# Reordering the opening of a one-core attention and feed-forward kernel: two quarters of q, the first bias loads, the mask's rows

## The chip, the cores and the metric

The kernel runs on one core of a Trainium2 chip. The metric is the device time of one execution in microseconds; the time of a kernel is the median of its runs. The engines work side by side and wait for each other by semaphores: TensorE (PE in the profile; PEld is its weight load), VectorE (DVE), ScalarE (ACT), GpSimd (POOL), and SyncE (SP), which here only issues DMAs.

## The reference

Eight sequences of 256 rows and 128 channels go through attention with 16 heads of 64 and a single k and v shared by the heads, then through a gated feed-forward layer with simulated 8-bit quantisation. The bias of the attention depends only on the distance between query and key and comes from a small network.

```python
xn = ln(x, g_norm)
q = (xn @ Wq).reshape(b, n, HEADS, DIM_HEAD).transpose(0, 2, 1, 3)
k, v = split(xn @ Wkv)                        # one head; a null key and a null value are put in front
q = l2norm(q) * q_scale;  k = l2norm(k) * k_scale
sim = einsum('bhid,bjd->bhij', q, k) * 8.0
bias = rel_pos_bias(...)                      # (heads, n, n), a Toeplitz matrix for each head
sim = where(causal, -inf, sim + [null_bias, bias])
sim = where(mask, sim, -inf)                  # mask of the keys, (b, n), all true in these inputs
out = softmax(sim) @ v
y = ln(out @ Wout, g_out)
x = x + ffn(y)                                # fake quantisation, w_gate, w_up, silu, w_down
```

## The kernel before

**Work and order.** The kernel is written by hand, engine by engine: each engine has one program, in the order of the code, and waits on named semaphores. No scheduler moves anything. After an opening that prepares the weights, the bias and the first sequence, a loop over 32 groups (8 sequences by 4 groups of 4 heads, `GB` = 4) does the attention; the last two groups are written out in `ending`, and the feed-forward part follows.

**The opening.** The q of the first sequence is made in four quarters (128 rows by 8 heads each; quarter `q` has rows `q % 2` and heads of half `q // 2`). A quarter goes through these steps: `q_make_first(q)` on PE (the product), `q_square(q)` on ACT, `q_norm2(q)` on DVE (the sum of squares for each head), `q_power(q)` on POOL (the power -1/2), `q_normalise(q)` on DVE (the product with it, into the one buffer `qn`), `qT_make(q)` on PE (four transposes of `qn` into the one bank `qT_ps`), and `qT_evac(q)` on DVE (the copy of `qT_ps` to `qT`). Quarter c may be normalised only when the transposes of quarter c - 1 are done, and be transposed only when the copy of quarter c - 1 is done. The first scores (`scores`, heads 0 and 1) need quarters 0 and 1, which are all rows of the first eight heads. `k_normalise` on DVE writes `kz`, which PE transposes (`kT_make`). `x_stats(1)`, `x_power(1)` and `x_normalise(1)` prepare the second sequence. `keep_busy(n, ...)` on PE transposes the unit matrix n times into a bank that nobody reads.

**The bias.** A table of 16 heads by 383 distances is computed, written to DRAM (`table_dram`) and read back by SP in eight DMAs of 256 KB: for each four heads, two blocks of keys. `ld_bias[k]` counts the two DMAs of heads 4k to 4k + 3. In group g of the first sequence, DVE waits for `ld_bias[g]` ahead of the first `score_pair`, which adds the bias to the scores of two heads and finds the row maxima, for ACT's `exponent`.

**The mask's rows.** `mrow` (one partition, bfloat16) holds an additive row of the mask for every sequence. ACT writes 2048 of its elements from the unsigned bytes of `mask_u`, DVE's `mask_tail` the other 1024. PE reads `mrow` only in the branch of the program that is taken when the mask has a zero; `least` picks the branch. With these inputs the other branch runs.

**GpSimd.** `x_power(0)`, `mlp_power(0)`, `mlp_power(1)`, `q_power(0, 0)` stand in that order; the `mlp_power`s belong to the small network that makes the bias. Later POOL multiplies the probabilities with the reciprocal sums (`normalise`).

Of the kernel before, what the change touches and what calls it, by code (L numbers as in the profile page):

```python
# [105 lines left out]
def held(eng, sem, value, passed):  # L106


    eng.wait_ge(sem, value)
    eng.sem_inc(passed, 1)  # L110
# [11 lines left out]
def build(nc, x, cond, mask, g_norm, Wq, Wkv, q_scale, k_scale, null_bias, w0, b0, g0, w1, b1, g1, w2, b2,  # L122
# [3 lines left out]
    with ExitStack() as ctx:  # L126
# [3 lines left out]
        def sem(name):  # L130
            return ctx.enter_context(nc.semaphore(name))
# [166 lines left out]
        ld_bias = [sem(f"ld_bias{k}") for k in range(4)]  # L298
        consts = sem("consts")
# [71 lines left out]
        def _(sp):  # L371
# [20 lines left out]
            for k in range(4):  # L392
                for blk in range(2):
                    toeplitz = bass.AP(table_dram, 4 * k * TABW + blk * P, [[1, P], [TABW, 4], [1, P]])
                    sp.dma_start(bias[:, 4 * k:4 * k + 4, blk * (P + 1) + 1:(blk + 1) * (P + 1)], toeplitz)\
                      .then_inc(ld_bias[k], 16)
# [29 lines left out]
        def _(pool):  # L426
# [25 lines left out]
            def x_power(n):  # L452
                power(mv[:, :, 1], rstd[:, :], n, 2, lambda: held(pool, x_aggr, 2 * (n + 1), pool_passed),
                      x_eps, x_rstd, True)
# [14 lines left out]
            def mlp_power(layer):  # L469
                power(mmv[:, :, 1], mrs[:, :], layer, 2, lambda: held(pool, mlp_aggr, 2 * (layer + 1), pool_passed),  # L470
                      mlp_eps, mlp_rstd, True)

            x_power(0)
            mlp_power(0)
            mlp_power(1)
# [62 lines left out]
        def _(act):  # L538
# [75 lines left out]
            q_square(3, q_ps0[3])  # L614
            act.wait_ge(ld_mask, 16)
            act.wait_ge(consts, 5)
            keys1 = mrow[0:1, :, 0:KEYS1].rearrange("p b (t k) -> p b t k", t=2)[:, :, :, 1:P + 1]
            mask_v = mask_u[:, :].rearrange("p (b n) -> p b n", b=B)[:, :, ::-1].rearrange("p b (t k) -> p b t k", t=2)
            act.activation(keys1, mask_v, ACT.Copy, scale=-NEG, bias=NEG).then_inc(mask_ready, 1)
            act.wait_ge(ld_v, 16 * 2)  # L620
            act.wait_ge(consts, 6)
            for a in range(2):
                for t in range(2):
                    dst = vnull[a * D:a * D + D, :, :].rearrange("p k h -> p (k h)")[:, 2 * a + t::2 * H + 4]
                    act.copy(dst, vcol[a * D:a * D + D, 0:1].broadcast_to([D, HP])).then_inc(vnull_ready, 1)

# [131 lines left out]
        def _(pe):  # L758
# [111 lines left out]
            keep_busy(4, idle)  # L870
# [5 lines left out]
            qT_make(0)  # L876
            q_make_first(3)
            keep_busy(6, idle)
            pe.wait_ge(null_a, 2)
            pe.wait_ge(kT_ready, 1)  # L880
            qT_make(1)
            keep_busy(6, idle)
# [314 lines left out]
        def _(dve):  # L1197
            def x_stats(n):
                for t in range(2):
                    dve.bn_stats(stat[:, t, :], X[:, 2 * n + t, :]).then_inc(x_stat, 1)  # L1200
                held(dve, x_stat, 2 * (n + 1), dve_passed)
                for t in range(2):
                    dve.bn_aggr(mv[:, t, :], stat[:, t, :]).then_inc(x_aggr, 1)

# [70 lines left out]
            def mask_tail():  # L1275

                mask_v = mask_u[:, :].rearrange("p (b n) -> p b n", b=B)
                dve.tensor_scalar(mrow[0:1, :, KEYS1 + 1:KEYS1 + P + 1], mask_v[:, :, ::-1][:, :, P:N], 1.0, -NEG,
                                  ALU.subtract, ALU.mult).then_inc(mask_ready, 1)

# [39 lines left out]
            mask_tail()  # L1320
            q_norm2(2, 2)
            qT_evac(0, 0, 0)
            q_normalise(1, 1, q_ps0[1])
            dve.wait_ge(ld_x, 16)
            x_stats(1)
            qT_evac(1, 1, 0)
            q_norm2(3, 3)
            q_normalise(2, 2, q_ps0[2])
# [97 lines left out]
            def group(s):  # L1426
# [16 lines left out]
                if s.at == 0:  # L1443
                    x_normalise(1)
                score_pair(heads(s.at)[2:4])
# [195 lines left out]
```

## Time and profile before

| | us |
|---|---|
| median of 3 runs | 286.36 |
| the three runs | 286.36, 286.25, 287.96 |
| profiled execution | 287.82 |
| its span in the profile | 285.9 |
| busy in it: PE, DVE, ACT, POOL | 260.6, 234.4, 223.5, 201.3 |

The rows of the trace are of the profiled execution, and count from the start of its span; 1.92 us of its time lie around the span. The profiled execution took 1.46 us more than the median of the runs, and lies near the slowest of them. In every row of a timeline the first two numbers are the start and the length in us; a row with x4 covers four instructions. "[0.94 <-DVE negmax L1379]" says that the engine had been idle for 0.94 us and what ended that. A DVE instruction can be shown starting up to 0.1 us before the one ahead of it has ended, so lengths of neighbours add up to a little more than the distance of their starts.

### The profile page before, as it was taken

To read this page: it belongs to the slowest core of one execution; us is meant where nothing else is said; L and a number is where in the kernel's file an instruction comes from. 1 tells how busy PE (TensorE), PEld (TensorE's weight loads), DVE (VectorE), ACT (ScalarE), POOL (GpSimd) and SP (SyncE) were. 2 spreads that over 40 slices of the span, in tenths; PEclk is the share of its full clock that TensorE was granted. 3 is DMA by queue.
4 is the path that set the end of the run, shared out by engine and by line. 5 is a ranking of instruction groups with operands and counts; after the bars stand their busy time and mean duration, and the time that the engine had idled before them with its cause. 6 is when DMAs were issued, how large, how long until landed. Compare 5 with 4: busy or idle time off the path is not lost.

```text
span 285.9 us, 7418 instructions
## 1 busy us (share of the span) xinstructions
PE 260.6 (91%) x2209; PEld 209.4 (73%) x2210; DVE 234.4 (82%) x973; ACT 223.5 (78%) x778; POOL 201.3 (70%) x395
## 2 busy tenths in 40 slices
PE   6889989999999999999999999999999999978261
PEld 5467768888788888888888888888888877752060
DVE  6699887998789888988898889787977787879893
ACT  3577878988898889888988898889888898358380
POOL 6485887887788778878887888778877785013310
PEclk9999999999999999999999999999999999999757
DMA  4746000000000000000000000000000200000004
GB/s 127 187 140 162 1 2 1 2 3 0 3 0 5 0 3 0 2 1 3 0 2 3 2 0 2 1 3 0 2 1 3 62 17 3 0 3 2 1 23 128
DMA packets 12109, 6.48 MB, mean 23 GB/s; under 512 B 1614, under 2 KB 11939, under 8 KB 12068
## 3 DMA queue, kind: packets, MB, share of 16 engines
q1 hardware_dynamic: 11642, 5.78, 7.8%
q8 instruction: 20, 0.33, 0.4%
q10 hardware_dynamic: 426, 0.20, 0.2%
q14 instruction: 21, 0.17, 0.2%
HBM read 4.88 MB, written 1.07 MB: 21 GB/s over the span
## 4 chain that ended last, share of the span: by engine, by line
PE 50%; DVE 17%; ACT 15%; POOL 8%; issue 7%; DMA 1%; DVEq 0%; POOLq 0%; ACTq 0%
PE bank L979 11%; ACT prob L633 8%; PE bank L930 7%; POOL rq L450 6%; PE back L1022 4%; PE front L956 4%; PE front L1022 4%; PE bank L793 4%; DVE score L1379 3%; PE back L956 3%; DVE qn L1243 3%; PE bank L811 3%; DVE qn L1237 2%; ACT sq L580 2%; DVE oT L1369 2%
## 5 line engine op out<-in xcount | busy, mean ns | idle before, releaser
L633 ACT ACTIVATE prob<-score,negmax 128x258 f32<-128x258 f32 (+1 forms) x256 | 113.9, 453 | 27.0 <-DVE negmax L1379 26.9
L491 POOL TENSOR_SCALAR prob<-prob,rrow 128x258 f32<-128x258 f32 x254 | 105.7, 436 | 22.2 <-DVE rrow L1387 19.2
L450 POOL TENSOR_TENSOR rq<-qn,neghalf 128x8 f32<-128x8 f32 x32 | 53.9, 1684 | 2.7
L979 PE MATMUL bank<-pT,val 128*64 128x256 f32 x496 | 49.9, 336 | 0.2
L633 ACT ACTIVATION_READ_ACCUMULATOR prob<-score,negmax 128x1 f32 x256 | 49.7, 194 | 0.0
L979 PEld LDWEIGHTS bank<-pT,val 128*64 128x64 f32 x496 | 30.2, 136 | 17.6 <-issue 4.9
L1379 DVE CUSTOM_DVE_ANT_0 score<-front,bias 128x258 f32<-128x258 f32 (+1 forms) x128 | 38.0, 353 | 2.0 <-PE front L956 1.8
L1243 DVE TENSOR_TENSOR qn<-bank,rq 128x512 f32<-128x512 f32 x31 | 21.3, 688 | 22.2 <-POOL rq L450 22.1
L930 PE MATMUL bank<-wout,oT 128*128 128x128 f32 x256 | 36.8, 287 | 2.1 <-DVE oT L1369 1.7
L1379 DVE CUSTOM_DVE_ANT_0 score<-back,bias 128x258 f32<-128x258 f32 (+1 forms) x128 | 37.3, 348 | 0.0
L930 PEld LDWEIGHTS bank<-wout,oT 128*128 128x128 f32 x256 | 30.9, 191 | 7.1 <-DVE oT L1369 5.2
L956 PE MATMUL front<-kT,qT 64*128 64x258 f32 (+1 forms) x256 | 29.7, 350 | 1.0 <-ACT pT L643 0.5
L1022 PE MATMUL front<-ident,prob 128*128 128x128 f32 x192 | 29.6, 273 | 0.0
L643 ACT COPY pT<-back 128x384 f32<-128x384 f32 x62 | 27.5, 490 | 2.1 <-PE back L1022 1.8
L956 PEld LDWEIGHTS front<-kT,qT 64*128 64x128 f32 x256 | 22.3, 186 | 7.9 <-issue 6.1
L1022 PE MATMUL back<-ident,prob 128*128 128x128 f32 x192 | 27.6, 274 | 0.1
L643 ACT COPY pT<-front 128x384 f32<-128x384 f32 x62 | 26.4, 470 | 1.3 <-PE front L1022 1.2
L1237 DVE TENSOR_REDUCE qn<-sq 128x8 f32<-128x512 f32 x32 | 21.7, 679 | 6.8 <-ACT sq L580 6.8
L956 PE MATMUL back<-kT,qT 64*128 64x258 f32 (+1 forms) x256 | 26.7, 326 | 0.0
L1369 DVE COPY oT<-bank 128x512 f32<-128x512 f32 x32 | 21.9, 684 | 3.5 <-PE bank L979 3.4
L1022 PEld LDWEIGHTS front<-ident,prob 128*128 128x128 f32 x192 | 22.8, 141 | 2.1 <-DVE negmax L1379 0.2
L956 PEld LDWEIGHTS back<-kT,qT 64*128 64x128 f32 x256 | 22.3, 187 | 1.8 <-issue 0.3
(228 smaller groups left out, 469.1 us busy)
## 6 DMA issues: line engine op xcount, KB each, us to landing
bias<-relative_table SPq DMA_DIRECT2D x8, 256.0 KB, 4.8
X<-in_x_dram SPq DMA_DIRECT2D x1, 896.0 KB, 5.7
out_dram<-prob SPq DMA_DIRECT2D x3, 256.0 KB, 2.6
prob<-in_L_cond_Wq_dram SPq DMA_DIRECT2D x1, 512.0 KB, 3.7
wout<-in_L_cond_Wout_dram SPq DMA_DIRECT2D x1, 512.0 KB, 5.6
prob<-in_L_ffn_w_down_dram SPq DMA_DIRECT2D x1, 176.0 KB, 4.0
X<-in_x_dram SPq DMA_DIRECT2D x1, 128.0 KB, 2.1
prob<-in_L_ffn_w_gate_dram SPq DMA_DIRECT2D x1, 128.0 KB, 2.1
```

The source lines that it names most:

```text
L450: pool.tensor_tensor(dst, src, neghalf[:, 0:width], ALU.pow).then_inc(done, 1)
L491: pool.tensor_scalar(prob[:, par, h, cols], prob[:, par, h, cols], rrow[:, par, h, t:t + 1], 1.0, ALU.mult, ALU.mult).then_inc(normed, 1)
L633: act.activation(prob[:, par, h, cols], score[:, h % 4, cols], ACT.Exp, scale=-1.0, bias=negmax[:, par, h, t:t + 1], accum_out=rowsum[:, p ...
L643: act.copy(pT[:, h % 4, :], bank[i][:, 0:3 * P]).then_inc(pT_ready, 1)
L930: pe.matmul(y_out(t), oT[:, m % 2, k, t * P:t * P + P], wout[:, k, :], start=k + t == 0, stop=False, skip_group_check=True)
L956: product = pe.matmul(banks[a][:, at:at + KEYS1 - c0], qT[par][rows, h // 2, t * P:t * P + P], kT[par][rows, c0:KEYS1], start=not masked, ...
L979: last = pe.matmul(ps[a * D:a * D + D, pair * N + i0:pair * N + N], val[m % 2][:, blk, :], turned[:, 2 * pair + a, c0:c1], start=blk == 1, ...
L1022: product = pe.transpose(bank[i][:, k * P:k * P + P], prob[:, par, h, c0:c0 + P], ident[:, :])
L1237: dve.tensor_reduce(qn2[:, q, :], sq[:, :, :], AX.X, ALU.add).then_inc(q_n2, 1)
L1243: dve.tensor_tensor(qn[:, :, :], ps[:, :].rearrange("p (h d) -> p h d", d=D), rq[:, q, :].unsqueeze(2).broadcast_to([P, 8, D]), ALU.mult). ...
L1369: dve.tensor_copy(oT[:, m % 2, 2 * g:2 * g + 2, :].rearrange("p k n -> p (k n)"), (q_ps if at == GB * B - 1 else val_ps)[:, :])\
L1379: dve.tensor_tensor_reduce(score[:, h % 4, c0:c0 + w], ps[:, c0:c0 + w], bias[:, h, 0:w], -1.0, -3.0 * NEG, ALU.add, ALU.min, negmax[:, pa ...
```

## The change

1. PE: `qT_make(0)` moves ahead of the transposes of `kz`, `qT_make(1)` ahead of the wait for `null_a` and `kT_ready`; sixteen `keep_busy` transposes in three lots become fifteen in four.
2. DVE: `mask_tail` is gone; `qT_evac(0)` now stands ahead of `q_norm2(2)`; `qT_evac(1)` moves into the middle of `x_stats(1)`, between its `bn_stats` and its `bn_aggr`; `q_normalise(2)` moves from ahead of the first pair of scores to behind it and `x_normalise(1)`. Ahead of the second pair there is a new wait for `ld_bias_pair`.
3. SP: the bias of heads 0 to 3 is loaded in four DMAs of 128 KB (heads 0 and 1, counted by `ld_bias[0]`, then heads 2 and 3, counted by `ld_bias_pair`) where there were two of 256 KB.
4. The mask's rows: both parts are now written by POOL, in `mask_rows`, between `mlp_power(0)` and `mlp_power(1)`.
5. ACT: its part of the mask's rows is gone, and `q_square(3)` stands behind the four copies to `vnull`, no longer ahead of them.

```diff
@@ SP
-            for k in range(4):
+            for h, count, loaded in ((0, 2, ld_bias[0]), (2, 2, ld_bias_pair), (4, 4, ld_bias[1]), (8, 4, ld_bias[2]),
+                                     (12, 4, ld_bias[3])):
                 for blk in range(2):
...
@@ POOL
+            def mask_rows():
+
+                pool.wait_ge(ld_mask, 16)
+                pool.wait_ge(consts, 5)
+                mask_v = mask_u[:, :].rearrange("p (b n) -> p b n", b=B)[:, :, ::-1]
+                keys1 = mrow[0:1, :, 0:KEYS1].rearrange("p b (t k) -> p b t k", t=2)[:, :, :, 1:P + 1]
+                for dst, src in ((keys1, mask_v.rearrange("p b (t k) -> p b t k", t=2)),
+                                 (mrow[0:1, :, KEYS1 + 1:KEYS1 + P + 1], mask_v[:, :, P:N])):
+                    pool.tensor_scalar(dst, src, 1.0, -NEG, ALU.subtract, ALU.mult).then_inc(mask_ready, 1)
+
             x_power(0)
             mlp_power(0)
+            mask_rows()
             mlp_power(1)
@@ ACT
             v_copy(0)
-            q_square(3, q_ps0[3])
-            act.wait_ge(ld_mask, 16)
-            act.wait_ge(consts, 5)
...
-            act.activation(keys1, mask_v, ACT.Copy, scale=-NEG, bias=NEG).then_inc(mask_ready, 1)
             act.wait_ge(ld_v, 16 * 2)
...
+            q_square(3, q_ps0[3])
@@ PE
-            keep_busy(4, idle)
+            keep_busy(3, idle)
+            qT_make(0)
+            keep_busy(3, idle)
             pe.wait_ge(kv_ready, 1)
             pe.wait_ge(kz_ready, 1)
             pe.transpose(misc[:, 2 * P:3 * P], kz[:, 2, :], ident[:, :])
             for t in range(2):
                 kT_make(0, t, halves(misc))
-            qT_make(0)
             q_make_first(3)
-            keep_busy(6, idle)
+            keep_busy(4, idle)
+            qT_make(1)
+            keep_busy(5, idle)
             pe.wait_ge(null_a, 2)
             pe.wait_ge(kT_ready, 1)
-            qT_make(1)
-            keep_busy(6, idle)
@@ DVE
             k_normalise(0)
-            mask_tail()
+            qT_evac(0, 0, 0)
             q_norm2(2, 2)
-            qT_evac(0, 0, 0)
             q_normalise(1, 1, q_ps0[1])
             dve.wait_ge(ld_x, 16)
-            x_stats(1)
+            x_stats_tiles(1)
             qT_evac(1, 1, 0)
+            x_stats_joined(1)
             q_norm2(3, 3)
-            q_normalise(2, 2, q_ps0[2])
...
                     x_normalise(1)
+                    q_normalise(2, 2, q_ps0[2])
+                    dve.wait_ge(ld_bias_pair, 16 * 2)
                 score_pair(heads(s.at)[2:4])
```

How the rows move on the engines follows, first of before, then of the change; the line numbers of the change are its own, some 8 to 15 higher. On PE, from the third quarter's product to the first scores (`bank<-ident,qn` is `qT_make`, `bank<-ident,kz` the transposes of `kz`, `back<-ident` is `keep_busy`, `bank<-prob` is `q_make_first(3)`, for `prob` lends its space to `wq` and `xT0`):

```order
L802 MATMUL bank<-prob 128x512
L869 TENSOR_LOAD mask_min
L818 MATMUL back<-ident 128x128 x4
L873 MATMUL bank<-ident,kz 128x128
L776 MATMUL bank<-ident,kz 128x128 x2
L811 MATMUL bank<-ident,qn 128x128 x4
L802 MATMUL bank<-prob 128x512
L818 MATMUL back<-ident 128x128 x6
L811 MATMUL bank<-ident,qn 128x128 x4
L818 MATMUL back<-ident 128x128 x6
L1185 COMPARE_AND_BRANCH
L956 MATMUL front<-kT,qT 128x258 x2
```

Of the change:

```order
L877 TENSOR_LOAD mask_min
L826 MATMUL back<-ident 128x128 x3
L819 MATMUL bank<-ident,qn 128x128 x4
L826 MATMUL back<-ident 128x128 x3
L883 MATMUL bank<-ident,kz 128x128
L784 MATMUL bank<-ident,kz 128x128 x2
L810 MATMUL bank<-prob 128x512
L826 MATMUL back<-ident 128x128 x4
L819 MATMUL bank<-ident,qn 128x128 x4
L826 MATMUL back<-ident 128x128 x5
L1194 COMPARE_AND_BRANCH
L965 MATMUL front<-kT,qT 128x258 x2
```

The first four `qn` transposes now stand ahead of those of `kz`; the second four have four `keep_busy` ahead of them, no longer six.

On DVE, from `k_normalise(0)` to the first score of the loop (`mrow<-mask_u` is `mask_tail`, `qT<-bank` is `qT_evac`, `qn<-sq` is `q_norm2`, `qn<-bank,rq` and `qn<-back,rq` are `q_normalise`, `score,negmax` is the score of one head and one half of the rows):

```order
L1226 SCALAR_TENSOR_TENSOR kz<-kv,rk,spread_keys 128x128 x2
L1278 TENSOR_SCALAR mrow<-mask_u 1x8x128
L1237 TENSOR_REDUCE qn<-sq 128x8
L1248 COPY qT<-bank 128x4x128
L1243 TENSOR_TENSOR qn<-back,rq 128x512
L1200 BN_STATS stat<-X 128x6 x2
L1203 BN_AGGR mv<-stat 128x2 x2
L1248 COPY qT<-bank 128x4x128
L1237 TENSOR_REDUCE qn<-sq 128x8
L1243 TENSOR_TENSOR qn<-bank,rq 128x512
L1379 ISA score,negmax<-front,bias 128x258
```

Of the change:

```order
L1241 SCALAR_TENSOR_TENSOR kz<-kv,rk,spread_keys 128x128 x2
L1263 COPY qT<-bank 128x4x128
L1252 TENSOR_REDUCE qn<-sq 128x8
L1258 TENSOR_TENSOR qn<-back,rq 128x512
L1209 BN_STATS stat<-X 128x6 x2
L1263 COPY qT<-bank 128x4x128
L1214 BN_AGGR mv<-stat 128x2 x2
L1252 TENSOR_REDUCE qn<-sq 128x8
L1387 ISA score,negmax<-front,bias 128x258
```

The mask's row has left, the first copy to `qT` has taken its place, the second stands ahead of `BN_AGGR`, and one `q_normalise` is gone from ahead of the scores. It stands here now, behind `x_normalise(1)` (`xn<-X,mv,rstd`):

```order
L1387 ISA score,negmax<-front,bias 128x129
L1387 ISA negmax 128x1
L1224 TENSOR_SCALAR xn<-X,mv,rstd 128x128 x2
L1258 TENSOR_TENSOR qn<-bank,rq 128x512
L1387 ISA score,negmax<-back,bias 128x258
L1387 ISA negmax 128x1
```

What follows that row is the second pair of scores, as before.

On POOL, between the powers of the small network's two layers (`mrs<-mmv,neghalf`):

```order
L446 TENSOR_SCALAR mmv<-mmv 128x2
L450 TENSOR_TENSOR mrs<-mmv,neghalf 128x2
L446 TENSOR_SCALAR mmv<-mmv 128x2
L450 TENSOR_TENSOR mrs<-mmv,neghalf 128x2
L448 TENSOR_SCALAR qn<-qn 128x8
```

Of the change:

```order
L448 TENSOR_SCALAR mmv<-mmv 128x2
L452 TENSOR_TENSOR mrs<-mmv,neghalf 128x2
L483 TENSOR_SCALAR mrow<-mask_u 1x8x2x128
L483 TENSOR_SCALAR mrow<-mask_u 1x8x128
L448 TENSOR_SCALAR mmv<-mmv 128x2
L452 TENSOR_TENSOR mrs<-mmv,neghalf 128x2
L450 TENSOR_SCALAR qn<-qn 128x8
```

Two instructions on one partition, of 2048 and 1024 elements, now stand ahead of `mlp_power(1)` and of all that follows on POOL.

## Rows read from the trace of the kernel before

**Rows 1.** Stage view: stretch, busy us of each engine, TensorE's clock, DMA share, GB/s.

```profile
20.00:30.00 10.00, 9.41 (x81) 7.97 (x80) 9.87 (x45) 8.24 (x34) 6.60 (x12) 1.00 0.66 162
```

**Rows 2.** Chain that ended last, in order of time: start us, us, what.

```profile
21.78 0.23 DVE score L1379
...
24.03 0.37 ACT xTh L552
...
24.68 3.37 ACT prob L633 x15
```

**Rows 3.** Timeline of DVE, 15 to 25.8 us.

```profile
16.33 0.68 DVE L1278 TENSOR_SCALAR mrow<-mask_u 1x1024 bf16<-1x1024 uint8 x1
...
17.55 0.69 DVE L1248 COPY qT<-bank 128x512 f32<-128x512 f32 x1
18.16 0.68 DVE L1243 TENSOR_TENSOR qn<-back,rq 128x512 f32<-128x512 f32 x1
18.75 0.47 DVE L1200 BATCH_NORM_STATS2 stat<-X 128x6 f32<-128x128 f32 x2
...
19.76 0.69 DVE L1248 COPY qT<-bank 128x512 f32<-128x512 f32 x1
...
21.78 0.43 DVE L1379 CUSTOM_DVE_ANT_0 score<-front,bias 128x258 f32<-128x258 f32 x1
...
22.90 0.60 DVE L1209 TENSOR_SCALAR xn<-X,mv,rstd 128x128 f32<-128x128 f32 x2
23.42 0.42 DVE L1379 CUSTOM_DVE_ANT_0 score<-back,bias 128x258 f32<-128x258 f32 x1
...
24.53 0.68 DVE L1248 COPY qT<-bank 128x512 f32<-128x512 f32 x1
```

**Rows 4.** Timeline of ACT, 16 to 24.6 us.

```profile
18.41 0.60 ACT L580 ACTIVATE sq<-bank 128x512 f32<-128x512 f32 x1 [0.60 <-PE bank L802]
18.90 1.90 ACT L619 ACTIVATE mrow<-mask_u 1x2048 bf16<-1x2048 uint8 x1
...
22.25 0.51 ACT L633 ACTIVATE prob<-score,negmax 128x258 f32<-128x258 f32 x1 [0.94 <-DVE negmax L1379]
```

**Rows 5.** Timeline of PE, 14 to 24 us.

```profile
16.91 0.60 PE L811 MATMUL bank<-ident,qn 128*128 128x128 f32 x4
...
19.10 0.63 PE L811 MATMUL bank<-ident,qn 128*128 128x128 f32 x4
...
20.60 0.93 PE L956 MATMUL front<-kT,qT 64*128 64x258 f32 x8 [0.22 <-DVE qT L1248]
```

**Rows 6.** Timeline of POOL, 5 to 30.4 us.

```profile
5.99 0.78 POOL L450 TENSOR_TENSOR mrs<-mmv,neghalf 128x2 f32<-128x2 f32 x1
10.93 0.19 POOL L446 TENSOR_SCALAR mmv<-mmv 128x2 f32<-128x2 f32 x1 [4.17 <-DVE mmv L1258]
...
15.80 1.67 POOL L450 TENSOR_TENSOR rq<-qn,neghalf 128x8 f32<-128x8 f32 x1
...
26.11 4.26 POOL L491 TENSOR_SCALAR prob<-prob,rrow 128x258 f32<-128x258 f32 x8 [2.83 <-DVE rrow L1387]
```

**Rows 7.** Timeline, 7.4 to 7.8 us.

```profile
7.63 1.19 DVE L1301 TENSOR_REDUCE mask_min<-mask_u 1x1 int32<-1x1024 uint16 x1
```

**Rows 8.** POOL's instructions by form: busy us in all, mean ns of one.

```profile
L491 POOL TENSOR_SCALAR prob<-prob,rrow 128x258 f32<-128x258 f32 x127 | 62.6, 493 | 22.2 <-DVE rrow L1387 19.2
...
L491 POOL TENSOR_SCALAR prob<-prob,rrow 128x129 f32<-128x129 f32 x127 | 48.1, 379 | 0.0
...
L440 POOL MEMSET wdp<- 128x384 bf16 x1 | 0.5, 548 | 0.0
```

**Rows 9.** Line 491: duration ns min/median/max, first and last start.

```profile
L491 POOL TENSOR_SCALAR prob<-prob,rrow x197: 369/480/1040, 26.1 to 199.6; 128x258 f32<-128x258 f32 x99, 128x129 f32<-128x129 f32 x98
```

**Rows 10.** SP's timeline from 14 us.

```profile
16.48 5.20 SPq L395 DMA_DIRECT2D bias<-relative_table  x8
```

**Rows 11.** The second and third bias DMA, issued from 16.9 and 17.4 us.

```profile
DMA to landing us min/median/max: 3.9/4.1/4.3
```

## What I expect of the change, before it ran

> **What bounds the kernel now.** I read the stage view first. From 20 to 30 us DVE is busy for 9.87 of 10.00 us, PE for 9.41, ACT for 8.24 and POOL for 6.60, with TensorE's clock at its full 2.4 GHz [rows 1]: this stretch goes at DVE's pace, and what helps it is less work on DVE, or fewer waits. The chain of waits, read next, says which work: it runs through DVE's first score at 21.78 us, ACT's evacuation of the second sequence (`xTh`) at 24.03, and then 3.37 us of exponentials without a gap [rows 2]. So two queues are close to each other there, DVE's and ACT's. Third comes DVE's own timeline, since the change is mostly an edit of it: from 16.33 us to the end of group 0's scores at 24.53 us the engine hardly stops [rows 3]. ACT, by contrast, waits 0.94 us for the first row maximum [rows 4]. Later POOL's `normalise` waits for DVE's reciprocals until 26.11 us and then works for 4.26 us at a stretch [rows 6].
>
> **The mask on DVE.** `mask_tail` starts at 16.33 us, and two instructions, it and `q_norm2(2)`, take until 17.55 us, so it holds DVE for 1.22 / 2 = 0.61 us [rows 3]. It goes, and nothing takes its place at that point if the first copy to `qT` is ready.
>
> **The first quarter's transposes.** The four take 0.60 us on PE [rows 5]. Before, they stood behind the transposes of `kz` and ended at 17.51 us, just in time for the copy at 17.55. Now they follow `q_normalise(0)`, which precedes `k_normalise(0)` on DVE, so by an estimate they are over by about 16.4 us, when DVE comes to the copy. I count no wait. The third lot of `keep_busy` is in front of `kz` only for as long as DVE makes it. DVE's order is then, with distances from [rows 3]: copy at 16.4, `q_norm2(2)` at 17.0, `q_normalise(1)` at 17.6 (it was at 18.16). POOL's power for that quarter runs from 15.80 for 1.67 us, to 17.47 [rows 6], so it doesn't hold it back; this is the first new wait to look for, with 0.1 us to spare.
>
> **The second quarter.** From the start of `q_normalise(1)` to that of its copy there were 19.76 - 18.16 = 1.60 us [rows 3], for the product, PE's transposes (0.63 us from 19.10 [rows 5]) and what lies between. `keep_busy` ahead of them is four long now, not six, and may save 0.1 of it. So the copy starts at 17.6 + 1.5 to 1.6 = 19.1 to 19.2 us, 0.6 us earlier. Part of the time won is a wait: the two `bn_stats` cover only 0.47 us [rows 3], and DVE then stands for some 0.4 to 0.5 us, since the aggregates, which used to fill part of it, now stand behind the copy. `q_square(3)` on ACT doesn't suffer: its product ends earlier, since `qT_make(0)` is out of its way, and the vnull copies that precede it now are over about when it started before, at 18.41 us [rows 4].
>
> **The first pair of scores.** PE's scores start 20.60 - 19.76 = 0.84 us after the copy does, and take 0.93 us [rows 5]: 20.0 to 20.9 us. DVE has the copy (0.6), the aggregates (some 0.3, estimate) and `q_norm2(3)` (0.6) to do, and comes to the scores at 20.7. With the first head's product ready shortly before the last, the first score starts at about 20.85 us, 0.93 us ahead of 21.78 [rows 3]. Here 0.6 of the gain is only moved: `q_normalise(2)` now comes later.
>
> **The bias in pieces.** SP issues its eight DMAs from 16.48 us, and they take it 5.20 us [rows 10]. The second and third, issued at about 16.9 and 17.4 us, landed 3.9 and 4.3 us later, at 20.8 and 21.7 [rows 11]. Heads 0 and 1 need only the first two pieces of 128 KB, so 20.8 us is an upper end for them, and they are needed at 20.85; by bytes they should land earlier, at about 20. Heads 2 and 3 have the bytes that landed by 20.8 before, plus two more issues (5.20 / 8 = 0.65 us each at most): 22.1 us at the latest, and they are needed at 23.1. The later heads get theirs some 1.3 us later at the worst, and are not needed before the second pair is through, at 24.2, and quarters 2 and 3 are copied behind it. So the pieces cost nothing; without them the first score would wait to 20.8, which is about the same. I price both waits at zero, and at 0.1 us at the outer end.
>
> Beside this, what a rule says: the Trainium skill ("DMA: Bandwidth & Descriptors", Bandwidth) wants DMAs of 1 MiB, and lists 138 GB/s for 64 KB and 341 GB/s for 1 MB. That speaks against the split. At 138 GB/s the four pieces would last 3.8 us in place of about 1.8. No row here shows a piece of 128 KB; if the rule held for pieces that stand in one queue, heads 2 and 3 would land around 23 us, and the sum would lose about 0.1 us.
>
> **Behind it.** The first pair takes 22.90 - 21.78 = 1.12 us, `x_normalise(1)` 0.52, `q_normalise(2)` about 0.6, the second pair 24.53 - 23.42 = 1.11 us [rows 3]. From 20.85 that is 22.0, 22.5, 23.1 and 24.2 us, against 24.53: 0.33 us. With the shorter path of the second quarter it is 0.43. **Term: -0.4 us.** As a check, DVE loses 0.61 us of work and gains about 0.2 us of standing. From there on the program is the same. The reciprocals, POOL's row of 4.26 us [rows 6] and the squares of the next quarter hang on DVE's queue, so they move by the same 0.4; the fixed arrivals, which are DMAs, have room. I let all of it through to the end.
>
> **ACT and PE.** ACT's 1.90 us for the mask [rows 4] buy nothing by themselves: 0.94 us of waiting follow them, which grow. ACT's evacuation of `xTh` moves 0.9 us up, though, with the first scores. PE does one idle transpose less; its clock is full in [rows 1], and the gaps change by tenths of a microsecond, so I expect the same clock.
>
> **The mask on POOL.** This is the open price. POOL is free from 5.99 + 0.78 = 6.77 us to 10.93, 4.16 us [rows 6], and then makes `mrs`, on which the bias table and the whole opening hang. The nearest rows are the `tensor_scalar` of 258 and of 129 elements: 493 and 379 ns [rows 8], so 114 / 129 = 0.88 ns for each element and 0.265 us fixed. With 2048 and 1024 elements this makes 2.07 + 1.17 = 3.24 us, over at 10.0; even had the mask landed only at 7.63, where DVE reads it without a wait [rows 7], it would be over at 10.9. Cost zero. Other rows are dearer: the bfloat16 memset took 548 ns for 384 elements, 1.43 ns each [rows 8], which makes 4.4 us and an end at 11.15, 0.2 late. The slowest of line 491 took 1040 ns where 493 is the mean of the longer form [rows 9], 2.1 times; that factor makes 6.8 us, an end at 13.6, 2.7 late. A gain is excluded, as POOL only gets work. I take zero, by the row of the same operation, and keep 2.7 as the end. Nobody waits for `mrow` itself in the branch that runs.
>
> **Sum.** -0.4 + 0 + 0 = -0.4 us. Against the profiled execution: 287.82 - 0.4 = 287.4. That one is 1.46 us above the median of the runs; the forecast is for a median: 286.36 - 0.4 = **286.0 us**. A measurement of this kernel can tell about 1%, 2.9 us, from no change.
>
> **The rivals.** *ACT's path decides.* If exponentials, not DVE, set the pace from 24 us on [rows 2], the full 0.93 us arrives: 285.4. DVE's 9.87 of 10 us speaks against it. *The loop swallows it.* If something that isn't shifted, or the rhythm of the groups, takes the gain back: 286.4. The same comes out if the second quarter waits longer for PE than I count, so that the change doesn't do what it is meant to. *POOL is late (slower).* The mask's bytes, read backwards and written as bfloat16 on one partition, take longer than the 258-element rows say. It decides from 4.16 us on, which is (4.16 - 0.53) / 3072 = 1.18 ns an element, a third more than 0.88. All that follows goes to the end one for one, for `mrs` was taken up by DVE at once. At the 2.7 us of the bound: 286.36 - 0.4 + 2.7 = 288.7. To pass 1% it would take 3.3 us. DVE is at work on other data at the time, and rows of 1040 ns exist, which speaks for it. *Another settling.* One run in three took 287.96 us, and so did about the profiled one. If the median of the changed kernel is such a run: 287.96 - 0.4 = 287.6. Nothing in the opening says which.
>
> **How the numbers follow.** Forecast (285.7 to 286.2) 0.52; ACT's path 0.12; swallowed 0.12; POOL late 0.14, of it 0.05 beyond 1%; another settling 0.10. 285.2 to 287.8 leaves out only the worse part of a late POOL and surprises. Faster by over 1% would need 2.9 us, which no case has: 0.03. Slower by over 1%: 0.06. Within: 0.91.
>
> **What would show it.** In the changed profile: POOL's two mask rows between 6.8 and 10.9 us, about 2.1 and 1.2 us, and `mmv` after them still at 10.9; `qT` copies on DVE at 16.4 and 19.1 to 19.2, with a wait of 0.4 us ahead of the second; the first score at 20.85, held by PE; the second pair over at 24.1 to 24.2 without a wait for the bias; POOL's first `normalise` at 25.7. I am wrong if POOL's rows pass 4.16 us, if DVE waits for the bias at either place, or if these times hold and the end doesn't move with them.

## The result: 3.3% slower, and the profile after

| | before | after |
|---|---|---|
| median of the runs made together | 286.35 us (6 runs, 286.00 to 287.96) | 296.89 us (6 runs, 295.66 to 297.72) |
| ratio, 95% interval | | 1.033, 1.029 to 1.037 |
| profiled execution, and its span | 287.82, 285.9 us | 296.12, 294.3 us |

The forecast was 286.0 us, with a range up to 287.8. The kernel takes 10.5 us more by the medians, and 8.4 us more by the spans of the two profiled executions. The 2 us between these two numbers belong to the runs and not to the change: the profiled execution of before is 1.47 us above its median, and the one of after 0.77 us below.

First, what ended last. The chain of waits of the changed kernel, some of its pieces up to 24 us (start us, us, what):

```profile
3.53 1.21 PE front L840 x4
7.00 5.43 POOL mrow L483
12.43 1.75 issue
14.18 3.62 POOL mrow L483
22.04 1.80 PE bank L810 x2
```

POOL's mask rows stand on the path, from 7.00 to 17.80 us. (The chain calls the end of the first row "issue"; the timeline has the row whole.) Their timeline, POOL from 6 us (start us, us, engine, line, operation; idle time before and its releaser in brackets):

```profile
6.13 0.79 POOL L452 TENSOR_TENSOR mrs<-mmv,neghalf 128x2 f32<-128x2 f32 x1
7.00 10.80 POOL L483 TENSOR_SCALAR mrow<-mask_u 1x2048 bf16<-1x2048 uint8 x2
17.88 0.19 POOL L448 TENSOR_SCALAR mmv<-mmv 128x2 f32<-128x2 f32 x1
```

The two instructions by themselves, from the view of their line (duration ns min/median/max, first and last start):

```profile
L483 POOL TENSOR_SCALAR mrow<-mask_u x2: 3624/5362/7100, 7.0 to 14.2; 1x2048 bf16<-1x2048 uint8 x1, 1x1024 bf16<-1x1024 uint8 x1
```

They take 7.10 and 3.62 us, from 7.00 to 17.80 us, where the forecast had 2.07 and 1.17. From the two sizes, 3.48 us for 1024 elements is 3.39 ns each, and 0.15 us fixed. `mmv`, which stood at 10.93 us with 4.17 us of idle time ahead of it [rows 6], now stands at 17.88 with none: 6.95 us late. DVE's timeline shows who waited, and where the planned order ended up:

```profile
18.90 0.73 DVE L1280 TENSOR_SCALAR prob<-front,mmv,mrs 128x128 f32<-128x128 f32 x2 [5.95 <-POOL mrs L452]
...
22.08 0.47 DVE L1323 TENSOR_SCALAR table<-front,b2c 16x256 f32<-16x256 f32 x1 [1.42 <-PE front L874]
...
24.64 0.69 DVE L1263 COPY qT<-bank 128x512 f32<-128x512 f32 x1 [0.71 <-PE bank L819]
...
27.27 0.69 DVE L1263 COPY qT<-bank 128x512 f32<-128x512 f32 x1 [0.36 <-PE bank L819]
...
29.70 0.43 DVE L1387 CUSTOM_DVE_ANT_0 score<-front,bias 128x258 f32<-128x258 f32 x1 [1.02 <-PE front L965]
...
31.34 0.68 DVE L1258 TENSOR_TENSOR qn<-bank,rq 128x512 f32<-128x512 f32 x1
31.94 0.42 DVE L1387 CUSTOM_DVE_ANT_0 score<-back,bias 128x258 f32<-128x258 f32 x1
```

Against [rows 3] the first score is 7.92 us later (29.70 - 21.78) and the second pair 8.52 us (31.94 - 23.42). So something has been added to the 6.95 us. The stage view (stretch, its length, busy us of PE, PEld, DVE, ACT and POOL, TensorE's clock, DMA share, GB/s) shows one part of it:

```profile
15.00:16.00 1.00, 0.00 (x0) 0.00 (x0) 0.00 (x0) 0.00 (x0) 1.00 (x1) 1.00 0.00 0
16.00:17.00 1.00, 0.00 (x0) 0.00 (x0) 0.00 (x0) 0.00 (x0) 1.00 (x1) 0.84 0.00 0
17.00:23.00 6.00, 3.30 (x9) 1.58 (x10) 2.68 (x11) 1.96 (x3) 5.50 (x9) 0.50 0.00 0
23.00:24.00 1.00, 1.00 (x5) 0.54 (x4) 0.93 (x4) 0.12 (x1) 1.00 (x1) 0.75 0.11 25
24.00:30.00 6.00, 5.65 (x43) 4.38 (x43) 3.99 (x10) 2.86 (x11) 3.59 (x8) 1.00 0.61 176
```

From 15 to 17 us POOL works alone. PE stood still from 13.2 to 19.68 us. Its granted clock went from full, 2.4 GHz, between 16 and 17 us to 1.2 GHz (0.50), and was there from 17 to 23 us, just when the delayed chain needed it. In the kernel before the same view has 1.00 from 10 to 24 us.

Last, does the shift reach the end? The first row of the closing stage on POOL, `sgu`, shows it, from the timeline of the changed kernel:

```profile
263.29 0.28 POOL L540 TENSOR_SCALAR sgu<-wsp,asc 128x10 f32<-128x10 f32 x1 [3.12 <-DVE asc L1539]
```

The same row of the kernel before:

```profile
254.77 0.28 POOL L527 TENSOR_SCALAR sgu<-wsp,asc 128x10 f32<-128x10 f32 x1 [3.12 <-DVE asc L1529]
```

The difference is 8.52 us, what it was at the second pair of scores 230 us earlier. This pair of rows, second pair and `sgu`, is the ruler of most experiments: the medians mix in an ending that varies by itself by 2 us (see the tail, below).

### The profile page after: what moved, and what is told of

It is laid out like the page before. It is cut to its first block, busy times and chain, and to the rows that moved or that the text cites. A ratio compares the mean times of both kernels' runs of the same rounds, so it can differ in the third digit from the quotient of the medians.

```text
span 294.3 us, 7419 instructions
## 1 busy us (share of the span) xinstructions
PE 263.8 (90%) x2209; PEld 210.9 (72%) x2209; DVE 235.9 (80%) x972; ACT 221.7 (75%) x777; POOL 211.8 (72%) x397
## 4 chain that ended last, share of the span: by engine, by line
PE 54%; DVE 15%; POOL 11%; ACT 10%; issue 7%; DMA 1%; DVEq 0%; POOLq 0%; ACTq 0%
PE bank L988 12%; PE bank L939 8%; PE front L965 5%; PE back L1031 5%; ACT prob L641 5%; POOL rq L452 5%; PE front L1031 4%; PE bank L801 4%; PE back L965 4%; PE bank L819 3%; POOL mrow L483 3%; DVE score L1387 3%; DVE qn L1258 2%; DVE oT L1377 2%; DVE qn L1252 2%
## 5 line engine op out<-in xcount | busy, mean ns | idle before, releaser
L641 ACT ACTIVATE prob<-score,negmax 128x258 f32<-128x258 f32 (+1 forms) x256 | 113.9, 453 | 29.6 <-DVE negmax L1387 29.5
L1258 DVE TENSOR_TENSOR qn<-bank,rq 128x512 f32<-128x512 f32 x31 | 21.3, 689 | 22.2 <-POOL rq L452 22.0
L1031 PE MATMUL front<-ident,prob 128*128 128x128 f32 x192 | 29.6, 273 | 0.0
```

The lines of the kernel that those rows point to most:

```text
L641: act.activation(prob[:, par, h, cols], score[:, h % 4, cols], ACT.Exp, scale=-1.0, bias=negmax[:, par, h, t:t + 1], accum_out=rowsum[:, p ...
L1031: product = pe.transpose(bank[i][:, k * P:k * P + P], prob[:, par, h, c0:c0 + P], ident[:, :])
L1258: dve.tensor_tensor(qn[:, :, :], ps[:, :].rearrange("p (h d) -> p h d", d=D), rq[:, q, :].unsqueeze(2).broadcast_to([P, 8, D]), ALU.mult). ...
```

## The experiments

Each ratio is to runs of the kernel before on the same chip. Shifts are against the profile of before: second pair 23.42 us, `sgu` 254.77 us.

**1. The order without the mask** (`e1_mask_back`). The changed kernel with `mask_tail` back on DVE and the other mask row back on ACT:

```diff
 mlp_power(0)
-mask_rows()
 mlp_power(1)
@@ ACT, behind q_square(3)
+act.activation(keys1, mask_v, ACT.Copy, scale=-NEG, bias=NEG)
@@ DVE
 k_normalise(0)
+mask_tail()
 qT_evac(0, 0, 0)
```

> The changed kernel, with the mask's rows again on ACT (behind the square of the fourth quarter) and on DVE (ahead of the first copy to qT), as before; the new order of the quarters and the bias in pieces stay. Theory 1, GpSimd's rows are the whole loss: 286.0 to 286.5 us, since the 0.6 us of the mask on DVE is back and little else changes. Theory 2, the new order or the pieces cost a wait of their own (the first score came 2.43 us after the second copy's start where 1.65 was forecast): 287 to 289 us, with DVE idle ahead of its first score by over 0.5 us.

Measured: 288.59 us against 288.01, ratio 1.003 (1.000 to 1.006). Second pair +0.35 us, `sgu` +0.37. The 8.5 us are gone, so they are the mask's. The time fell into the range of theory 2, and DVE did stand idle for 0.61 us ahead of its first score; but at `sgu` that costs only 0.37 us. (The median is high because 9 of the 10 runs took over 288.4 us, where 7 of the 13 of the kernel before took over 287.5; see experiment 9.) What remains is a small loss, where a small gain was forecast.

**2. The mask alone** (`e2_mask_only`). The kernel before, with only the mask's rows on POOL (its `mask_tail` and ACT's row removed).

> The kernel before with one part of the change alone, the mask's rows on GpSimd between the two powers of the small network. Theory 1: the two rows take 7.1 and 3.6 us again, mmv after them starts near 17.9 us, and the time is 296 to 297 us, as with the whole change. Theory 2: 293 to 295 us, the rest being the order's and the pieces'.

Measured: 295.88 us, ratio 1.028 (1.024 to 1.032). Its rows take the same 10.80 us, the second pair is at 31.06 (+7.64) and `sgu` at 262.42 (+7.65). With experiment 1 this puts nearly all of the slowdown on `mask_rows` from both sides. The changed kernel is another 0.87 us behind it at `sgu`. Here too the clock is at 0.50 from 17 to 23 us, and `mmv` starts 6.89 us late; so in the old order the end is only 0.76 us later than `mmv`, in the new one 1.57 us (8.52 - 6.95).

**3. The clock** (`e3_kept_busy`). The changed kernel, with idle transposes on PE through POOL's rows:

```diff
+keep_busy(54, idle)
 mlp_turn(1)
 keep_busy(3, idle)
```

> The changed kernel with 54 more transposes of the unit matrix on PE ahead of the second layer's turn, to fill the time in which it stood idle. Theory 3, the low clock behind the stall (0.50 from 17 to 23.7 us) cost some of the loss: granted clock 1.00 through the opening and 1.0 to 1.5 us less than the changed kernel, 295.4 to 295.9 us. Rival, the low clock lay beside other waits: 296.9 us, unchanged.

Measured: 294.04 us, ratio 1.021 (1.017 to 1.025). Its stage view, with the columns as above:

```profile
15.00:17.00 2.00, 2.00 (x21) 2.00 (x19) 0.00 (x0) 0.00 (x0) 2.00 (x1) 1.00 0.04 8
17.00:23.00 6.00, 4.59 (x31) 3.18 (x30) 3.46 (x14) 2.60 (x5) 5.50 (x9) 1.00 0.02 4
```

The clock stays full. The bias table is at 21.30 us in place of 22.08, the first score at 28.20 in place of 29.70, and `sgu` at 261.78 in place of 263.29: 1.51 us. POOL's rows begin 0.11 us earlier here (6.89 us), so some 1.4 us are the clock's, in this order. In the old order it can't be that much, since all that came on top there was 0.76 us (experiment 2). The wait on POOL so cost more than its own length. The median fell by more than the 1.0 to 1.5 us that were expected, 2.85 us; 1.5 of it is there at `sgu`, and in the profiled executions 1.0 us more lies behind it, in the ending.

**4. What makes the rows slow** (`e4_rates`, then `e8_rates2`). Both append rows to POOL's program in an otherwise unchanged kernel, so their times in all say nothing. The first keeps the pair subtract, multiply of `mask_rows` and changes the direction, the source's type and the destination's; its last row is a plain copy with a cast.

> The kernel before with eight more instructions on GpSimd at its very end, behind all other work, on one partition, each waiting for the one ahead: the mask's conversion of 2048 bytes read backwards, then of 1024 backwards, 1024 forwards, 1024 float32 to bfloat16, 1024 bytes to float32, 1024 float32 to float32 forwards and backwards, and a plain copy of 1024 bytes to bfloat16. One look, for the durations. If reading bytes is what is dear, the float32 reads take 1.2 us and the byte reads 3.6; if writing bfloat16 is, the reverse; if reading backwards is, the forward ones take 1.2 us; if it is the access pattern on one partition, all take 3.6 us.

POOL's timeline (each instruction asked for alone, so that rows of one form stand apart):

```profile
281.44 7.10 POOL L550 TENSOR_SCALAR mrow<-mask_u 1x2048 bf16<-1x2048 uint8 x1 [2.18 <-DVE prob L1620]
288.63 3.63 POOL L550 TENSOR_SCALAR mrow<-mask_u 1x1024 bf16<-1x1024 uint8 x1
292.34 3.63 POOL L550 TENSOR_SCALAR mrow<-mask_u 1x1024 bf16<-1x1024 uint8 x1
...
303.46 3.62 POOL L550 TENSOR_SCALAR scr<-X 1x1024 f32<-1x1024 f32 x1
...
310.85 1.03 POOL L560 CAST mrow<-mask_u 1x1024 bf16<-1x1024 uint8 x1
```

Backwards (288.63) and forwards (292.34), bytes to bfloat16 and float32 to float32 (303.46): always 3.62 to 3.63 us for 1024 elements. The copy from bytes to bfloat16 takes 1.03. So it is neither the bytes, nor the direction, nor the format, which is what the rival of the prediction had blamed. The expectation would have read "all take 3.6 us" as the single partition; the second kernel, with 128 partitions, shows that it isn't that either. What the slow rows share is their operations, and those the second kernel varies, on 1024 float32 of `X`:

```diff
+one(1, 1.0, -NEG, ALU.subtract, ALU.mult)   # 281.77
+one(P, 1.0, -NEG, ALU.subtract, ALU.mult)
+one(P, 1.0, 2.0, ALU.subtract, ALU.mult)    # 289.23
+one(P, 1.0, 2.0, ALU.add, ALU.mult)         # 292.94
+one(P, 1.0, 2.0, ALU.mult, ALU.mult)
+one(1, 1.0, 2.0, ALU.mult, ALU.mult)
+one(P, 1.0, 2.0, ALU.mult, ALU.add)         # 296.32
+one(P, 2.0, None, ALU.mult, None)           # 297.44
+one(P, 2.0, None, ALU.subtract, None)       # 300.31
+one(P, asc[:, 0:1], 1.0, ALU.mult, ALU.mult) # 303.18
```

> The kernel before with ten more instructions on GpSimd at its end, each over one run of 1024 float32 elements: subtract and multiply by constants on 1 and on 128 partitions, with a huge and a small factor, then add and multiply, multiply and multiply (128 and 1 partitions), multiply and add, one multiplication, one subtraction, and multiply by a column and by 1. One look, for the durations. All five forms of the first look but the plain copy took 3.6 us, so neither bytes nor bfloat16 nor the direction is dear. If the operation is (subtract first), the multiply and multiply rows take 1.2 us; if constants in place of a column are, only the last row does; if it is the single partition, only the rows on 128 do; if the huge factor is, the rows with 2.0 are fast.

POOL's timeline; the order is that of the diff, the numbers there are the starts here:

```profile
281.77 3.64 POOL L545 TENSOR_SCALAR oT<-X 1x1024 f32<-1x1024 f32 x1 [2.58 <-DVE prob L1615]
...
289.23 3.63 POOL L545 TENSOR_SCALAR oT<-X 128x1024 f32<-128x1024 f32 x1
292.94 1.04 POOL L545 TENSOR_SCALAR oT<-X 128x1024 f32<-128x1024 f32 x1
294.07 1.05 POOL L545 TENSOR_SCALAR oT<-X 128x1024 f32<-128x1024 f32 x1
...
296.32 1.04 POOL L545 TENSOR_SCALAR oT<-X 128x1024 f32<-128x1024 f32 x1
297.44 2.78 POOL L545 TENSOR_SCALAR oT<-X 128x1024 f32<-128x1024 f32 x1
300.31 2.77 POOL L545 TENSOR_SCALAR oT<-X 128x1024 f32<-128x1024 f32 x1
303.18 1.12 POOL L545 TENSOR_SCALAR oT<-X,asc 128x1024 f32<-128x1024 f32 x1
```

Pairs of add and multiply take 1.04 to 1.05 us, the pair that begins with a subtraction 3.63 to 3.65, whatever the factor or the number of partitions, and a single operation 2.77 to 2.78. The last row is the operation of line 491, whose rows gave the forecast its price: it is one of the fast pairs.

Beside this, a rule: the Trainium skill ("GPSIMD Engine Reference", 3.1 Elementwise, side-by-side cycle accounting) gives 1.03 cycles for each element as long as k is at most 2, and doesn't say what k counts. If it is the operations, that is at the 1.2 GHz of the page an estimate of 0.88 us for 1024 elements. The add and multiply pairs are within a fifth of it; the subtraction, at 3.63 us, and the single operation, at 2.77, are not.

**5. The mask's rows with an addition** (`e11_add`). x - 1 is x + (-1):

```diff
-pool.tensor_scalar(dst, src, 1.0, -NEG, ALU.subtract, ALU.mult)
+pool.tensor_scalar(dst, src, -1.0, -NEG, ALU.add, ALU.mult)
```

> The changed kernel with one word of the mask's rows other: they add -1 and multiply, where the change subtracts 1 and multiplies, which gives the same numbers. In the durations of the second look, a row of 1024 took 3.63 us with subtract first and 1.04 us with add first. Theory 1: the two rows take about 2.0 and 1.05 us, mmv starts at 10.9 us again, the clock stays at 1.00 in the opening, and what is left is the new order's own effect, as with the mask on ACT: second pair of scores from 23.7, sgu row near 255.1, 286.0 to 288.7 us. Rival: bytes on one partition in this place stay dear (over 4.16 us together), and the time stays above 289 us.

POOL's timeline:

```profile
6.83 3.01 POOL L483 TENSOR_SCALAR mrow<-mask_u 1x2048 bf16<-1x2048 uint8 x2
10.91 0.19 POOL L448 TENSOR_SCALAR mmv<-mmv 128x2 f32<-128x2 f32 x1 [1.06 <-DVE mmv L1273]
```

3.01 us, over at 9.84, and `mmv` at 10.91 with 1.06 us to spare. Measured: 288.00 us, ratio 1.002 (0.999 to 1.005), `sgu` at 254.89, +0.12 us. One operator was the whole of the slowdown, but for these 0.12 us.

**6. The mask's rows on ACT alone** (`e5_tail_on_act`). The changed order, nothing of the mask on POOL; ACT writes the small row too, behind its first `wqh` product.

> The changed kernel with no mask work on GpSimd and none on DVE: ACT writes the 1024 elements in its gap behind the first half of wqh, and the 2048 behind the square of the fourth quarter. This is the change as the forecast's -0.4 us was meant, without the dear rows. By the forecast's own steps: copies to qT at 16.4 and 19.1 us, first score at 20.85, second pair from 23.1 (before: 23.42), and the scales of the feed-forward part (POOL's sgu row) 0.3 to 0.4 us earlier than before's 254.77. Rival, from the run with the mask put back, which stood 0.37 us behind before at that row although its DVE did the same work: the order itself costs, and sgu is no earlier than 254.7. The time then also hangs on where the clock of the last 30 us rises, 286.0 to 288.6 us in either case.

Measured: 286.78 us against 287.82, ratio 0.999 (0.996 to 1.002); second pair 23.69 (+0.27), `sgu` 255.09 (+0.32). The first score came at 21.45 us, where 20.85 was expected. With the mask's rows off DVE and POOL the order still loses a little. So the forecast's term of -0.4 us is wrong in its sign, by itself.

**7. The pieces alone** (`e6_pieces_only`). The kernel before with the bias of heads 0 to 3 in four DMAs, and the wait.

> The kernel before with one part of the change alone, the bias of the first four heads in four DMAs of 128 KB and the wait for the second pair's. No theory gives it a price: DVE's first score at 21.8 and its second pair at 23.4 us as before, sgu at 254.8 (within 0.1), time 286.0 to 288.4 us. If the pieces cost a wait, it shows ahead of the first score or of the second pair.

First score 21.82, second pair 23.46, `sgu` 254.82: +0.04 to +0.05 us, all of which `mmv` has already (10.99 in place of 10.93). The pieces cost nothing in the opening. The ratio is 1.003 (1.001 to 1.006), which the rows up to `sgu` don't explain; what differs is how often the ending falls long, in 10 of 11 runs here and in 14 of 25 of the kernel before (experiment 9). Whether the pieces have a part in that is not shown; experiment 6, which has them too, fell long in 4 of 10.

**8. The order of DVE around the first pair** (`e12_quarter_ahead`, `e13_norm_behind`). Both start from experiment 5. The first moves `q_normalise(2)` back ahead of the first pair of scores; the second puts `q_norm2(3)` behind that pair instead, so that the sums that POOL's next clamp reads come later.

```diff
@@ e12
 q_norm2(3, 3)
+q_normalise(2, 2, q_ps0[2])
 ... first pair of scores
 x_normalise(1)
-q_normalise(2, 2, q_ps0[2])
@@ e13
-q_norm2(3, 3)
 ... first pair of scores
+q_norm2(3, 3)
```

> As the run before (add -1), and the third quarter's q_normalise back ahead of the first pair of scores on DVE, where the kernel before had it. DVE stood idle for 1.03 us ahead of its first score in the run with the mask on ACT, and did this row of 0.6 us behind it. Theory 4, the moved row is what costs in the new order: first score at 21.1 to 21.5 us, second pair from 22.8 to 23.1 (before: 23.42), sgu row 0.3 to 0.6 us ahead of before's, at 254.2 to 254.5. Rival, the first score moves back by the same 0.6: second pair from 23.7, sgu at 255.1.

> As the first run of this call (add -1), and q_norm2(3) on DVE behind the first pair of scores, so that GpSimd's clamp for that quarter doesn't stand near the first score. One look. In three runs the first score started 1.59 to 1.61 us behind the start of PE's scores and 0.09 behind that clamp's end, in one 1.19 us behind PE and ahead of the clamp. If it is GpSimd's instruction that holds DVE's first score, it starts 1.2 us behind PE's scores, at about 21.0 us. If it is PE or the bias, it stays at 21.4 to 21.5.

Of each kernel the start of PE's scores, and what DVE does until its first. Experiment 5, DVE then PE:

```profile
21.35 0.43 DVE L1387 CUSTOM_DVE_ANT_0 score<-front,bias 128x258 f32<-128x258 f32 x1 [1.01 <-PE front L965]
```

```profile
19.76 0.93 PE L965 MATMUL front<-kT,qT 64*128 64x258 f32 x8 [0.33 <-DVE qT L1263]
```

`q_normalise(2)` back ahead, DVE:

```profile
19.00 0.69 DVE L1263 COPY qT<-bank 128x512 f32<-128x512 f32 x1 [0.35 <-PE bank L819]
...
20.33 0.68 DVE L1258 TENSOR_TENSOR qn<-bank,rq 128x512 f32<-128x512 f32 x1
21.01 0.43 DVE L1388 CUSTOM_DVE_ANT_0 score<-front,bias 128x258 f32<-128x258 f32 x1
```

`q_norm2(3)` behind, DVE:

```profile
21.46 0.43 DVE L1386 CUSTOM_DVE_ANT_0 score<-front,bias 128x258 f32<-128x258 f32 x1 [1.58 <-PE front L965]
```

With 0.6 us more work ahead of it, the first score comes 0.34 us *earlier* (21.01 against 21.35), and the second pair at 22.65, -0.77 us against before; `sgu` is at 254.00, -0.77, all of it a little better than expected. The median is 287.35, ratio 1.001 (0.998 to 1.003). With less work ahead (`e13`, one execution, 288.83 us) the first score is at 21.46, no earlier, the second pair at 24.29 (+0.87) and `sgu` at 255.60 (+0.83).

From the start of PE's scores to DVE's first score it is 1.18 us in the kernel before (20.60 to 21.78), 1.18 in `e12` and in experiment 2, and 1.17 in experiment 7, `e9` and `e14` (below), where DVE has work until 0.2 us before it or less. Where it stands idle ahead of the score it is 1.59 in the changed kernel and in experiment 5, 1.60, 1.61 and 1.58 in experiments 6, 3 and `e13`. Experiment 1 doesn't fit: 1.19 with 0.61 us idle, although DVE began to wait 0.58 us after the start of PE's scores, exactly as in experiment 5. So idleness alone doesn't set it. `e13` was made for one explanation, that POOL's clamp of the next sums, which ran during the wait, holds the score back. It moved that clamp to 23.46 us, and the wait stayed: that explanation falls. The bias falls too: its first two pieces had landed by 20.1 us in both experiment 5 and `e12`. What makes these 0.4 us is open.

**9. The ending** (`e9_tail_busy`, `e14_ahead_and_tail`). From `sgu` to the end of the span it is 31.1 us in the kernel before and 31.0 after, but 29.6 in experiment 7 and 30.0 in experiment 3, with one program from there on. The 25 to 29 runs of the kernel before in a session fall in two groups, 285.9 to 286.8 and 287.6 to 288.9 us. The profiled execution of before and that of experiment 7 are one of each. Their stage views, before then experiment 7:

```profile
270.00:274.00 4.00, 0.85 (x5) 0.56 (x6) 3.25 (x12) 2.09 (x5) 0.00 (x0) 0.50 0.00 0
...
276.00:278.00 2.00, 1.90 (x19) 1.64 (x18) 1.83 (x4) 1.72 (x4) 0.09 (x1) 0.50 0.00 0
```

```profile
276.00:278.00 2.00, 1.90 (x29) 1.64 (x28) 2.00 (x5) 1.78 (x4) 0.03 (x1) 0.84 0.00 0
```

PE is nearly idle in the last normalisation and its clock is at half. When the down products come (from 273.6 us), it rises at about 276.6 us in experiment 7 and only at 278.6 in the kernel before, and the same 36 products take 3.96 and 4.58 us. The idle transposes of `e9_tail_busy` are for this stretch:

```diff
+keep_busy(34, qT_ps)
 over_partitions(1)
+keep_busy(24, qT_ps)
```

> The kernel before with 34 transposes of the unit matrix on PE ahead of the second spread of the maximum and 24 behind it, in the 4.2 and 3.1 us in which PE stood idle in the last 20 us. In five profiles the stretch from the sgu row to the end took 30.0 to 31.6 us, by where the granted clock rose again in it. Theory 3, the clock there is what makes times differ by up to 1.6 us beyond what the opening does: clock 1.00 through the down products, their row of 4.58 us down to about 4.0, the stretch 29.4 to 29.9 us and the time 284.6 to 285.5 us in all runs. Rival, the spread comes from elsewhere: 286.0 to 288.4 us in two groups as before.

In the kernel before they keep the clock at 1.00 until PE's last product, and the stage from `sgu` to DVE's last row shrinks from 26.84 to 25.82 us. The median is 286.50, ratio 0.997 (0.995 to 1.000). The forecast of 284.6 to 285.5 us in all runs failed, and the two groups remain (285.95 to 286.58 and 287.54 to 287.96 us): the profiled execution took 287.96 us and lost the microsecond behind DVE, in its last stores, 5.5 us in place of 4.3. So the clock is one part of the spread, and the last DMAs are another, which I didn't separate further.

> As e12, and PE kept busy by 34 and 24 transposes of the unit matrix in its two idle stretches near the end, as in e9, where DVE's last row came 25.8 us behind the sgu row, not 26.8 as in the profile of before. The two gains add: sgu at 254.2 to 254.5, DVE's last row at 280.0 to 280.4, and some 1 us or 0.3% less than before at the same end of the stores, 285.0 to 287.3 us.

`e14_ahead_and_tail`, experiment `e12` and these transposes together: 285.67 us (12 runs, 285.15 to 287.09) against 287.65, ratio 0.996 (0.993 to 0.999), `sgu` at 254.00 and the end of DVE's last row at 279.8. It is the fastest kernel of the study, 0.4% faster than the kernel before.

## Why the prediction was wrong, step by step

- **"The mask on POOL" failed**, and with it the forecast. It priced the rows at 0.88 ns an element and 0.265 us, "by the row of the same operation". Line 491 multiplies twice; `mask_rows` subtracts and multiplies. For the fast pairs the price was right to a tenth: 3.24 us forecast, 3.01 in experiment 5. For the pair in the diff it is 3.39 ns and 0.15 us: 10.72 us of work where 4.16 were free, and with the gaps between instructions `mmv` comes 6.95 us late. The upper bound, 2.7 us late, came from the slowest row of line 491 and from a memset; no row of before had this pair in it at length, and none of the bounds reached it.
- **The rival "POOL is late"** named the right place. Its point of decision, 4.16 us of work, fits the runs: rows of 3.01 us cost nothing, rows of 10.72 us delayed `mmv`. "One for one to the end" does not hold from `mmv` on: 6.95 us became 8.52, and 6.89 became 7.65. It holds from the second pair of scores on. Its reason (bytes, backwards, bfloat16, one partition) is refuted by experiment 4, and its price was two and a half times too low.
- **"I expect the same clock" failed** as a consequence. For small gaps it holds (1.00 in experiments 1 and 5); when PE had stood from 13.2 us on, it had half its clock from 17 us, worth some 1.4 us. 6.95 + 0.12 (the order, experiment 5) + 1.4 = 8.5 us, which is what `sgu` shows. This sum holds for the new order; the old order lost only 0.76 us on top of `mmv`'s delay at the same low clock, so clock and order are not two independent prices. Which wait makes the difference was not tested.
- **The copies to `qT`** were right: 16.4 and 19.1 to 19.2 us forecast, with a wait of 0.4; 16.30 and 18.92 in experiment 5, with 0.36. They are 1.25 and 0.84 us earlier than before.
- **"The first pair of scores" was mis-sized.** It let the first score start 0.85 us after PE's first product, before the products were over. The row of before has 1.18 us (20.60 to 21.78 [rows 3, 5]), and I had taken it for DVE's own business, since `q_normalise(2)` ran until then. 21.35 us was measured against 20.85 forecast. Since 0.6 us of work had been moved behind it, the term of -0.4 us became +0.1 to +0.3. The cover mattered: back in its place, that work fits into the wait, and the order gives -0.77 us (experiment `e12`).
- **The bias in pieces at zero** was right: in the changed kernel the four pieces landed 2.9, 3.4, 3.3 and 3.4 us after their issue at 24.1, 24.5, 25.0 and 25.5, so the two of heads 0 and 1 by 27.9 us, 1.8 us ahead of the first score, and those of heads 2 and 3 by 28.9, 3.0 us ahead of the second pair. By the estimate that the prediction made from the rule of the Trainium skill ("DMA: Bandwidth & Descriptors", Bandwidth) heads 2 and 3 would have landed around 23 us; in experiment 5 they had by 21.3. That table is of DMAs issued from GpSimd, and these are SP's. Experiment 7 shows no cost above 0.05 us.
- **"I let all of it through to the end"** was right to 0.05 us in every kernel, counted from the second pair of scores to `sgu`: +8.52 and +8.52, +7.64 and +7.65, +0.35 and +0.37, -0.77 and -0.77. The rivals "ACT's path" and "the loop swallows it" had no part in it.
- **"Another settling"** is real in the kernel before (experiment 9): its profiled execution is one of the slower group and its median one of the faster, which is 1.5 of the 2 us between the two differences of the result. For the changed kernel, with six runs of 295.66 to 297.72 us, groups are not shown.

## What to carry to other kernels

A rate is that of an operation with its operands: take the price of a moved instruction only from a row with the same operators, and where no row has them, the bound must be as wide as that ignorance, above all when the instruction goes onto a queue with a chain behind it. Of an engine that seems late because it was busy, ask when its input was ready; work ahead of a wait is free, and moving it behind the wait makes it cost its full length. To see a gain under 1%, compare a row late in the program but ahead of the stage that varies, and not the medians alone.

## What the runs showed of the hardware

- `tensor_scalar` on POOL, 1024 elements: add and multiply pairs 1.04 us, subtract and multiply 3.63 us, one operation alone 2.77 us, a copy with a cast 1.03 us. Two operations are faster than one. Partitions (1 or 128), direction and types changed nothing.
- PE had no work from 13.2 us on; between 16 and 17 us TensorE's clock fell from 2.4 to 1.2 GHz. It stayed there until after 23 us, when PE had worked again since 19.68. That cost some 1.4 us in the changed kernel, on top of the stall.
- A DVE instruction that stands beside POOL's first mask row took 2.68 us where it took 0.20 before. The timeline of the changed kernel:

```profile
8.90 2.68 DVE L1312 SCALAR_TENSOR_TENSOR prob<-prob 1x64 f32<-1x64 f32 x1
```

  It starts within POOL's row of 7.00 to 14.10 us, and ends at 11.58, ahead of that row's end. Experiments 2 and 3 have the same 2.68 us. In experiment 5 it is 0.20 us again, but there it starts at 8.74 us, between POOL's two rows (6.83 to 8.73, and from 8.81). The Trainium skill ("GPSIMD Engine Reference", Specifications) says that VectorE and GpSimd share their SBUF interfaces and contend where VectorE has two inputs in SBUF, which this instruction has. The 2.68 us agree with that, but no run separates it from other causes. It was never on the path, since POOL was busy until 17.80 us anyway.
- A DVE that had stood idle took the first score 1.58 to 1.61 us after PE's first product, in five kernels, and one that came from other work 1.17 to 1.18, in six. Experiment 1 (1.19, idle) breaks the pattern, and the cause is open.
